# Context products moved into the attention drain, small constants loaded early, and a grouped feed-forward cut into a half and two quarters

## The reference, cut to what matters

```python
x = x + tanh(g_xattn[0]) * attention(layernorm(x), ctx)     # 32 query heads, 8 key/value heads of 128
x = x + tanh(g_ffn[0])   * grouped_ffn(layernorm(x))        # features permuted, 16 groups of 32:
                                                            # up 32 -> 128, exact gelu, down 128 -> 32, unpermuted
x = x + tanh(g_xattn[1]) * group_attention(layernorm(x), ctx, ctx)
x = x + tanh(g_ffn[1])   * expert_ffn(layernorm(x))         # one of 8 experts a token, by argmax

# group_attention(q, k, v), per block of 128 x 512:
t, p, g = Wt @ v, Wp @ q, Wg @ k
att = sum over a group of 16 rows and 512 columns of p * g
y   = Wz (block diagonal) @ (att * t);   out = groupnorm(y) * gn_w + gn_b + v
```

## Time and profile before

| | us |
|---|---|
| median of 3 runs | 853.31 |
| lowest and highest | 850.31, 854.73 |
| the profiled execution | 851.44 |
| its span, first to last instruction | 849.7 |

### The profile page before, as it was taken

How to read it: one execution, slowest core, us unless ns; L and a number is a source line. 1 busy time by engine, 2 the same in 40 slices (tenths; PEclk the granted TensorE clock), 3 DMA queues, 4 the chain that set the end, 5 groups by cost and what they waited for, 6 DMA issues and landing times. The chain is left out here.

```text
span 849.7 us, 13807 instructions
## 1 busy us (share of the span) xinstructions
PE 770.1 (91%) x3850; PEld 605.1 (71%) x3850; DVE 484.1 (57%) x885; ACT 489.3 (58%) x1840; POOL 338.5 (40%) x639
## 2 busy tenths in 40 slices
PE   5999958999999999999999999999988888678990
PEld 3888846888888887888887888888876333255760
DVE  4775304556556555565565655655666456646773
ACT  4543217776766765766666676676552655334760
POOL 0330014443443444344353453453232455125883
PEclk9999979999999999999999999999999898867995
DMA  8435641021021021012002003000021577513436
GB/s 293 146 123 159 186 132 62 15 74 63 14 73 65 14 74 64 13 33 103 13 28 98 24 12 111 25 12 14 1 100 49 182 254 307 192 50 125 148 128 218
DMA packets 46151, 80.66 MB, mean 95 GB/s; under 512 B 5128, under 2 KB 25608, under 8 KB 42640
## 3 DMA queue, kind: packets, MB, share of 16 engines
q1 hardware_dynamic: 43536, 71.66, 24.8%
q0 software_dynamic: 2560, 8.39, 3.0%
HBM read 55.40 MB, written 24.64 MB: 94 GB/s over the span
## 5 line engine op out<-in xcount | busy, mean ns | idle before, releaser
L552 ACT ACTIVATE p_sb<-p_sb,nmax 128x128 f32<-128x128 f32 x256 | 99.7, 391 | 132.0 <-DVE nmax L698 132.0
L626 POOL TENSOR_TENSOR v_lo<-v_raw,v_hi 128x128 fp32r<-128x128 f32 x64 | 29.6, 462 | 258.2 <-ACT v_hi L590 258.2
L721 DVE TENSOR_TENSOR pT_lo<-bank,pT_hi 128x512 fp32r<-128x512 f32 x64 | 44.2, 691 | 48.9 <-ACT pT_hi L565 48.9
L763 PEld LDWEIGHTS bank<-kT,qT_sb 128*128 128x128 f32 x512 | 66.9, 191 | 7.1 <-ACT qT_sb L560 1.8
L631 POOL TENSOR_TENSOR p_sb<-p_sb,rsum 128x512 f32<-128x512 f32 x64 | 66.6, 1041 | 6.6 <-DVE rsum L717 6.6
L763 PE MATMUL bank<-kT,qT_sb 128*128 128x128 f32 x512 | 67.6, 275 | 1.4 <-ACT qT_sb L560 1.4
L597 ACT ACTIVATE q_junk<-bank 128x128 f32<-128x128 f32 x256 | 66.1, 272 | 4.2 <-PE bank L775 4.2
L689 DVE TENSOR_TENSOR oT_lo<-bank,oT_hi 128x512 fp32r<-128x512 f32 x64 | 44.0, 688 | 36.3 <-ACT oT_hi L547 36.3
L547 ACT ACTIVATE oT_hi<-bank 128x512 fp32r<-128x512 f32 x64 | 38.1, 595 | 40.2 <-PE bank L814 35.8
L392 PE MATMUL bank<-w_hi,ctx_hi 128*128 128x512 f32 x128 | 53.8, 420 | 7.6 <-DVE ctx_lo L323 7.6
L727 DVE SCALAR_TENSOR_TENSOR x_sb<-bank,tgates,x_sb 128x512 f32<-128x512 f32 x64 | 48.0, 751 | 22.0 <-PE bank L803 22.0
(11 more groups left out here) (259 smaller groups left out, 2163.8 us busy)
## 6 DMA issues: line engine op xcount, KB each, us to landing
w_raw<-in_wq_l SPq DMA_DIRECT2D x8, 1024.0 KB, 5.5
w_raw<-in_wo_l SPq DMA_DIRECT2D x8, 1024.0 KB, 4.8
exp_w<-in_exp_w_l SPq DMA_DIRECT2D x8, 1024.0 KB, 11.9
kT_scr<-kT_st SPq DMA_DIRECT2D x16, 256.0 KB, 2.3
v_scr<-v_st SPq DMA_DIRECT2D x16, 256.0 KB, 2.6
sorted_x<-ctx_nat SPq DMA_DIRECT2D x1, 3840.0 KB, 11.9
hid<-sorted_x SPq DMA_DIRECT2D x15, 256.0 KB, 2.7
sorted_y<-ctx_nat SPq DMA_DIRECT2D x15, 256.0 KB, 2.1
```

What stands on the lines that cost most here:

```text
L552: last = act.activation(p_sb[:, b % 2, h * P:(h + 1) * P], p_sb[:, b % 2, h * P:(h + 1) * P], ACT.Exp, bias=nmax[:, b % 2, h:h + 1], accum ...
L763: last = pe.matmul(s_ps[:, h * P:(h + 1) * P], qT_sb[:, b % 2, h * P:(h + 1) * P], kT[:, b * P:(b + 1) * P], start=True, stop=True)
```

## The change

Five things are changed together.

1. The ten constants are issued right after `x` at the start of `project_kv`. SP no longer waits for them; PE does, before its first product of attention.
2. `ctx_nat` and `g` change places in memory. `ctx_nat` now lies over `w_lo` (even heads) and is loaded as soon as head 6 is through. `z` 0 to 3 are made inside attention's last steps (stages `z01`, `z2`, `z3` on PE, `copy_z01`, `copy_z2`, `copy_z3` on ACT, banks 0, 3, 0, 1); output projection of unit 61 waits for the first two copies. `z` 4 to 7 take the place of `z` 0 to 3 in `middle`, ACT copies 4 and 5, DVE 6 and 7.
3. PSUM is declared as four pairs of banks. `up` writes two heads into the two banks of a pair, over three pairs in turn, and one GELU instruction reads both banks (`[128, 2, n]`).
4. The second half of the tokens is cut into two quarters of 256 tokens: 12 packs instead of 8, and 12 scatters. `yT_scr` has three parts, and statistics, seeds, shifts and normalisation go by `THIRDS` (blocks 0 to 3, 4 and 5, 6 and 7).
5. Orders: the statistics of `z` stand between the `yT` copies on DVE; `g` 0 and 1 follow the last `down`; all eight expert weights are issued after the last `yU` load; POOL waits for the context before its scatters.

```diff
@@ project_kv, SP
             sp.dma_start(s.x[:, :, :], d.x).then_inc(x_ld, 16)
+            for dst, src in ((s.up[:, :, :], d.up), ... (s.gn_b[:, :], d.gn_b)):
+                sp.dma_start(dst, src).then_inc(s.mid_ld, 16)
...
-            for dst, src in ((s.up[:, :, :], d.up), ... (s.gn_b[:, :], d.gn_b)):
-                sp.dma_start(dst, src).then_inc(mid_ld, 16)
             for i in range(3):
                 sp.wait_ge(first_ld[i], 48)
             sp.wait_ge(wo_ld, 16)
-            sp.wait_ge(mid_ld, 160)
@@ attention, SP
+            sp.wait_ge(q_done, 8 * G - 8)
+            sp.wait_ge(o_done, 8 * G - 8)
+            sp.dma_start(s.ctx_nat[:, :, :], d.ctx).then_inc(s.ctx_nat_ld, 16)
+            sp.wait_ge(o_done, UNITS)
@@ attention, ACT
+            def copy_z01(u, b, g, odd):
+                if after(u, b, g, B - 2):
+                    copy_z(0, 1)
...
-            run(act, [(oT_split, -2), (exps, 0), (qT_copy, 1), (pT_split, -1), (v_split, 2), (q_stats, 2), ...
+            run(act, [(oT_split, -2), (exps, 0), (copy_z01, 0), (qT_copy, 1), (pT_split, -1), (copy_z2, -1), (copy_z3, -1),
+                      (v_split, 2), (q_stats, 2), (seed_ln2, -3), (copy_xT, -6)]
@@ attention, PE
+                if after(u, b, g, B - 3):
+                    pe.wait_ge(s.z_copied[1], 2)
...
+            def z01(u, b, g, odd):
+                if after(u, b, g, B - 2):
+                    pe.wait_ge(s.ctx_nat_ld, 16)
+                    pe.wait_ge(q_scaled, u + 1)
+                    pe.wait_ge(acc_done, u - 2)
+                    z_product(0)
+                    z_product(1)
...
+            pe.wait_ge(s.mid_ld, 16 * 10)
             pe.matmul(oT_ps[:, 0:P], s.wt[:, :], s.wzT[:, :], start=True, stop=True).then_inc(mT_done, 1)
+            run(pe, [(scores, 0), (q_proj, 2), (z01, 0), (q_transpose, 1), (p_transpose, -1), (z3, -1), (o_proj, -2),
+                     (z2, -1), (values, -1), (transpose_x, -5)])
@@ middle, ACT
-            for n in range(PACKS):
-                reached(act, down_done, n - 1)
-                for i in range(HG):
-                    act.wait_ge(up_done, HG * n + i + 1)
-                    act.activation(hid[:, HG * (n % 2) + i, :], up_ps[i][:, :], ACT.Gelu).then_inc(gelu_done, 1)
+            for k in range(PACKS):
+                toks = pack(k)[1]
+                reached(act, down_done, hidden_free(k))
+                for j in range(2):
+                    act.wait_ge(up_done, 4 * k + 2 * j + 2)
+                    act.activation(hidden(k, j), up_ps[(2 * k + j) % 3][:, :, 0:toks.stop - toks.start], ACT.Gelu)\
+                        .then_inc(gelu_done, 1)
...
-            for b in range(HB, B):
-                copy_z(b)
-            for b in range(3):
+            for b in range(5):
                 copy_g(b)
             seed3(0)
+            copy_g(5)
+            copy_g(6)
             normalise3(0)
-            copy_g(3)
-            copy_g(4)
+            copy_g(7)
             seed3(1)
-            for b in (5, 6, 7):
-                copy_g(b)
             normalise3(1)
+            seed3(2)
+            normalise3(2)
@@ middle, POOL
-            for n in range(KT):
-                scatter(n)
             pool.wait_ge(ctx_nat_ld, 16)
             pool.wait_ge(col_step, 2)
-            scale_ctx(range(HB))
-            for n in range(KT, PACKS):
-                scatter(n)
-            scale_ctx(range(HB, HB + 2))
+            for jt in range(KT):
+                scatter(0, jt)
+            scale_ctx(range(2))
+            for jt in range(KT):
+                scatter(1, jt)
+            for jt in range(KT):
+                scatter(2, jt)
+            scale_ctx(range(2, HB))
             rstd3(0)
-            scale_ctx(range(HB + 2, B))
-            add_ctx(range(3))
+            scale_ctx(range(HB, B))
+            add_ctx(range(2))
             rstd3(1)
+            add_ctx(range(2, 3))
+            rstd3(2)
             add_ctx(range(3, B))
@@ middle, DVE
+            updates_with_stats(dve, s, update_x, x_done, bn_done, mv_done, xval3_done, THIRDS[1:2])
+            updates_with_stats(dve, s, update_x, x_done, bn_done, mv_done, xval3_done, THIRDS[2:3])
+            shift(1)
             for b in range(B):
-                if b == 1:
-                    shift(1)
+                if b == 2:
+                    shift(2)
@@ middle, PE
-            pe.wait_ge(z_copied[0], HB)
+            pe.wait_ge(z_copied[1], HB + 2)
...
+                        pe.matmul(up_ps[(2 * k + i // 2) % 3][:, i % 2, 0:toks.stop - toks.start], s.up[rows, jt, :],
+                                  xg[rows, jt, toks], start=True, stop=True).then_inc(up_done, 1)
...
+            for b in range(2):
+                g_product(b)
+            pe.wait_ge(yT_copied, PACKS)
             for b in range(HB):
                 transpose_y(b)
...
+            for b in range(2, 6):
+                g_product(b)
+            transpose_y(4)
+            transpose_y(5)
+            g_product(6)
             p_product(0)
+            transpose_y(6)
+            transpose_y(7)
+            g_product(7)
             p_product(1)
```

243 lines of the change are left out of this document (126 added, 117 removed).

## The result

The changed kernel takes **839.38 us** (median of four runs, 838.81 to 840.56) against 853.21 us of the kernel before beside it. The ratio is 0.9844, its 95% interval 0.9815 to 0.9872. So it is faster by 1.6%, 13.3 us (11 to 16), and 8.9 us slower than the 830.5 forecast; the range ended at 839.

What follows compares the result with a forecast made beforehand. PE is 91% busy; the middle is bound by POOL, transfers and hand-overs. Seam 8.6 + drain 1.1 + middle 11.9 = 21.6 us off 851.44 gives 829.8, from the median 831.7; forecast 830.5 (826 to 834), wider range 824 to 839.

Steps and rivals of the forecast that it cites:

- Constants early: Seam before attention: SP through at 113.2 us instead of 119.7, 6.5 us gained; 8.6 us with the clock's share.
- The 2.1 from the clock: Seam before attention: PE's pause shrinks from 8.71 to about 2.2 us and the clock stays up, worth 2.1 us.
- Drain: End of attention: z products fill PE's pauses and the clock holds; 1.1 us earlier, bounds 1.3 and minus 1.
- Feed-forward and POOL: Middle: last packs end at 681.7 instead of 687.4; POOL's 1.25 us transfers bind, last scatter issued 687.6 instead of 689.84.
- The middle's 11.9: Feed-forward through tail: a_col comes 11.9 us earlier, bounds 7 and 15.
- the chain of the forecast: Middle: gathers, POOL's scatters back to back, landing, yU loads, then normalisation rounds to a_col, 11.9 us earlier.
- Landing: Middle's last scatter: lands in 2.7 us, not 7.5, with two expert weights gone from there; 690.3 instead of 697.3.
- GELU: Feed-forward on ACT: one instruction over two heads costs 1.03 us.
- TensorE stays at 1.2 GHz: Rival, 835 us, chance 0.12: clock stays down at seam, in drain and under last products; gain shrinks by 5.
- the seam's part: Within the clock rival: clock stays down at the seam before attention, losing 2.1 us; whole rival's chance 0.12.

Runs made afterwards that it cites:

- both_filled: seam_filled plus 24 unread products of 512 columns in PE's pauses of the experts' routing; 845.86 us (ratio 0.9911).
- before_wait_early: Kernel before, with SP's wait for the last output projection put ahead of its xT_scr stores; 853.22 us against 853.44 (ratio 1.0003).
- stores_free_again: stores_free run a second time, in the third sitting; 841.87 us (ratio 0.9855).
- gap_filled_short: Changed kernel plus four unread products ahead of PE's wait for the first gather; 842.18 us (ratio 0.9863).
- exp_w_between: Changed kernel with the loads of expert weights 0 and 1 put back behind the first yU load; 840.86 us (ratio 0.9845).
- stores_free: Changed kernel with SP's wait for the last output projection moved back behind the first xT_scr stores; first sitting 836.05 us (ratio 0.9797).
- seam_filled: stores_free plus eight unread products of 512 columns at the end of PE's K/V stage; 834.50 us (ratio 0.9777).
- seam_filled_again: seam_filled run a second time, in the last sitting; 841.22 us (ratio 0.9847).

## Why the prediction was right or wrong

*Constants early: mechanism right, the clock's share not.* Of the 8.6 us, the 6.5 from SP came. The 2.1 from the clock were a matter of the execution. All kernels with early constants and without filled pauses at the seam start attention at 113.1 to 114.9 us; then between 0 and 16 passes of the first units ran 0.43 apart and not 0.23, and the lead at unit 63 was 5.4 to 10.1 us (6.5 in the changed kernel's first profile; the K/V stage's own end, which varies by some 1.5 us, is in it). I had taken a pause of 2.92 us in the drain, which the clock survived, as evidence for the pause of 2.3. The seam has three pauses, and the later two brought it down too: both_filled fell at 124 us with the first one filled. The ten early issues took SP 10.1 us (9.89 to 20.0 us of the span) and not 4.4; SP's last value stores came 0.7 us sooner all the same, so they were covered.

*Drain: right.* 1.3 us against 1.1, clock 1.00, the context in time.

*Feed-forward and POOL: wrong, and here the forecast failed.* "Every pack is ready before its scatter. POOL's rate of issue, not GELU, is the bound now, and it hides up to 5 us of slowness in the feed-forward." Two things were wrong in it. The kernel before already spoke against the rate of issue: there four of the eight scatters waited for a pack, 6.4 us in all, as this row does, which I passed over:

```profile
677.80 0.97 POOL L994 DMA_INDIRECT yT_scr<-xg,perm_col  x1 [2.34 <-DVE xg L1073]
```

First the input was late. The list of the parts left out the wait for the last output projection, which now precedes the stores. It costs 3.3 us at the first gather's issue and 1.2 more at its landing; PE's first `up` comes 10.1 us after the middle's first z product (8.4 before), against 6.8 in all nine executions with the stores freed. In the kernel before the same wait shows no cost (before_wait_early).

Secondly the cover is not 5 us. PE transposes the first half's `yU` only behind the last pack's copy, so the tail hangs on the last `down` product as well as on the scatters. From that product to `a_col` it took 30.2 to 30.6 us in 13 of the 17 profiled executions of kernels with the new middle (681.77 to 711.98 here, 684.33 to 714.59 in stores_free_again), whatever the scatters did, and 30.9 to 32.1 in the other four. By my own numbers the last `down` was at 681.7 and `a_col` at 713.0: a cover of 1.1 us. It came 7.9 us late on the forecast's clock, and `a_col` 6.8. The middle's 11.9 became 5.1. Of the 7.9, 4.3 were there at the first GELU; some 3.6 came on top between it and the last `down`, and no run takes these apart.

Where the stores were free and no stall came (three executions, all of the first two sittings), the middle gave 11.0, 9.8 and 7.9 us. So the chain of the forecast exists, but it is the best case of a stage in which a late landing, the stall and the clock each take a part. What the stall is and why it came in the last three sittings is open. What the freed stores are worth in whole time is open for the same reason: 4.8 us in the first sitting, and in the third nothing that can be seen (841.87 us against 842.18 of gap_filled_short, which keeps the wait). Packets of the instruction queues fall into that stretch in some executions and not in others, and not at the stall's place in all, so I don't name them as the cause. No run tried it. Nor did a run take back the quarters or the new place of the z products alone, so what each of them is worth is argued and not measured.

*The half clock in the first packs* explained nothing by itself (gap_filled_short: 65.3 us for the middle without it), though the windows show 0.56 and 0.58 just where the packs were slow.

*Landing: near in size, wrong in worth.* The median is 2.7 us, the last scatter took 3.6 against 2.7 forecast and 7.5 before; but exp_w_between puts the loads back, and nothing changes.

*GELU: right.* 0.97 us for 1024 columns (2.91 for three) against 1.03 taken.

*The rivals.* Of "TensorE stays at 1.2 GHz" the seam's part came true in some executions (the changed kernel's first profile among them). The place of the real loss stood in no rival. "The forecast is wrong if `a_col` comes less than 7 us nearer to the start of the middle": it came 5.1 nearer.

## What to carry to other kernels

Go through a change's waits one by one, also those that only moved: for each, what is queued behind it on its engine, and what covered it before. Here another edit of the same change took the cover away.

"Hidden behind X" needs both chains followed to the point where they meet. I followed POOL's to the tail and not PE's, whose program order ties the tail to the last pack.

If one execution in a profile agrees with a theory, run it in a second sitting before believing its size, and look whether what disturbs it goes by sitting. stores_free took 836.1 and 841.9 us in two, while the kernel before stayed at 853.1 and 853.4.

A row that says "remote" or "issue" is no proof that an engine stopped by itself. Look at what the engine waits for, and whether a third engine (DVE here) is late by the same products.

## What the runs showed of the hardware

- An unread f32 product of 512 columns costs PE 0.87 us (36 passes in 15.69), one of 128 columns 0.25 (18 passes in 2.25), one of 512 columns in the K/V stage's split type 0.23 to 0.25 (eight in 1.98). Only the short ones fit into pauses of 0.5 to 2 us; in the routing they held the clock at 1.00.
- The clock fell in pauses of 0.7 to 2.4 us in some executions and in others of the same kernel not. In seam_filled no pass was slow; in both_filled, the same up to there, seven were.
- In six of nine executions with the stores freed, all of the last three sittings, ScalarE waited 3.2 to 4.5 us for TensorE's count ahead of a GELU of pack 4 or 5, where PE's rows have the products done earlier (by 2.7 us in seam_filled_again).
- A gather landed 3.5 us after its issue where only the first half's stores had run before it (stores_free), and 4.8 to 6.3 us where it ran beside the second half's stores (the changed kernel's first four).
- One GELU over two banks, 1024 columns, took 0.97 us, two of 512 columns 1.01.
